# Six constant bf16 products per attention slot, behind the third weighing

## The reference

```
x = x + jnp.tanh(g_xattn[1]) * _L1_xattn_ref(_layernorm(x), ctx_1024, ctx_1024, ...)
x = x + jnp.tanh(g_ffn[1])   * _L1_ffn_ref(_layernorm(x), ...)      # tanh(h W A1 A2 + bias)
x = x + jnp.tanh(g_xattn[2]) * _L2_xattn_ref(_layernorm(x), ctx_1024, ...)
# in both: q, k, v projections, heads of 16, softmax(q k^T / 4) v, output projection
```

## Time and profile before

| what | value |
|---|---|
| median of 3 runs | 1412.94 us |
| lowest and highest run | 1395.23 and 1415.35 us |
| the profiled execution, its own time | 1407.57 us |
| its span in the trace | 1405.8 us |
| PE busy in the span | 1226.4 us, 87% |
| DVE, ACT busy | 716.4 and 450.6 us |
| granted TensorE clock, mean | 0.917 |

### The profile page before, as it was taken

How to read it: one execution, slowest core, us unless ns; L and a number is a source line. 1 busy time by engine, 2 the same in 40 slices (tenths; PEclk the granted TensorE clock), 3 DMA queues, 4 the chain that set the end, 5 groups by cost and what they waited for, 6 DMA issues and landing times.

```text
span 1405.8 us, 19389 instructions
## 1 busy us (share of the span) xinstructions
PE 1226.4 (87%) x6360; PEld 764.1 (54%) x6361; DVE 716.4 (51%) x2061; ACT 450.6 (32%) x842; POOL 293.8 (21%) x347
## 2 busy tenths in 40 slices
PE   6999999999879989998988669999567698999984
PEld 4534434434434443543443649999556446877862
DVE  7263473468966545644752531111376742545557
ACT  3322223123544354444434113333242211333320
POOL 2111111130030011001000041111113662355560
PEclk9999999999987998999998579999876799999997
DMA  9999999100000000000100845555229223455538
GB/s 304 337 337 327 332 335 315 46 1 1 1 0 1 1 1 1 1 1 1 33 1 1 262 145 201 178 175 180 103 77 329 90 91 116 118 152 158 149 108 306
DMA packets 140424, 186.75 MB, mean 133 GB/s; under 512 B 8672, under 2 KB 124896, under 8 KB 140224
## 3 DMA queue, kind: packets, MB, share of 16 engines
q1 hardware_dynamic: 130800, 159.28, 36.8%
q0 software_dynamic: 9552, 26.52, 5.1%
HBM read 83.71 MB, written 102.06 MB: 132 GB/s over the span
## 4 chain that ended last, share of the span: by engine, by line
PE 66%; DVE 15%; issue 7%; ACT 4%; DMA 3%; SPq 2%; POOL 2%; another core or an unknown queue 0%; DVEq 0%; POOLq 0%; ACTq 0%
PE psum L1979 13%; PE psum L1258 6%; PE psum L1269 6%; PE psum L2191 5%; PE psum L2248 3%; PE psum L930 2%; PE psum L2225 2%; PE psum L2272 2%; DVE arena L2810 2%; PE psum L2169 2%; PE psum L1972 2%; PE psum L2007 2%; PE psum L941 2%; ACT xn L1735 2%; PE psum L1933 1%
## 5 line engine op out<-in xcount | busy, mean ns | idle before, releaser
L1979 PE MATMUL psum<-arena 128*128 128x512 f32 x432 | 198.6, 609 | 0.0
L2810 DVE TENSOR_REDUCE arena<-psum 128x4 f32<-128x616 f32 x128 | 101.6, 797 | 100.8 <-PE psum L2191 99.4
L1979 PEld LDWEIGHTS psum<-arena 128*128 128x128 f32 x432 | 80.3, 192 | 113.9 <-issue 113.1
L2191 PE MATMUL psum<-arena 32*128 32x308 f32 x512 | 104.2, 502 | 19.2 <-DVE arena L2810 17.8
L1176 POOL DMA_INDIRECT ys<-xnT,arena x96 | 92.4, 962 | 104.7 <-DVE xnT L1153 82.1
L2392 ACT ACTIVATE arena<-psum,arena 128x512 f32<-128x512 f32 x72 | 49.1, 686 | 166.2 <-PE psum L1979 156.5
L1870 POOL TENSOR_TENSOR x_tok<-x_tok,add_row 128x1024 f32<-128x1024 f32 x16 | 38.3, 2400 | 289.6 <-ACT xn L1735 289.5
L2483 ACT ACTIVATE arena<-psum 128x2048 f32<-128x2048 f32 x40 | 74.9, 1874 | 63.3 <-PE psum L2229 46.6
L1049 PE MATMUL psum<-arena,xn 128*128 x384 | 87.1, 380 | 2.3 <-ACT xn L1099 1.9
L1258 PEld LDWEIGHTS psum<-side,arena 128*128 128x128 f32 x736 | 87.1, 195 | 2.7 <-ACT side L1303 1.6
L1258 PE MATMUL psum<-side,arena 128*128 128x128 f32 x736 | 87.5, 278 | 1.0 <-ACT side L1303 1.0
(11 more groups left out here) (408 smaller groups left out, 2092.6 us busy)
## 6 DMA issues: line engine op xcount, KB each, us to landing
xs<-zeros SPq DMA_DIRECT2D x8, 8576.0 KB, 59.7
arena<-in_W SPq DMA_DIRECT2D x31, 1024.0 KB, 12.0
xn<-xs SPq DMA_DIRECT2D x64, 134.0 KB
arena<-in_gate_up SPq DMA_DIRECT2D x4, 2048.0 KB
arena<-ys SPq DMA_DIRECT2D x4, 2048.0 KB, 14.7
arena<-xs SPq DMA_DIRECT2D x32, 134.0 KB
arena<-in_down SPq DMA_DIRECT2D x4, 1024.0 KB, 5.4
xs<-zeros SPq DMA_DIRECT2D x1, 2990.0 KB, 17.8
```

The costliest lines, as they stand in the source:

```text
L1979: ins = pe.matmul(bank[dict(hn=4, r=5, z=6, xn=7)[k]][:], lhs[:, cols], r, start=(start and n == 0), stop=(stop and n == len(w) - 1))
L2191: ins = pe.matmul(bank[most_bank(n, k) + i][:, 0:2 * M].rearrange("p (h m) -> p h m", h=2), qhT[rows, n % 3, c, t * P:(t + 1) * P], keys[r ...
L2810: dve.tensor_reduce(neg[:, n % 2, t, 2 * pair:2 * pair + 2, 2 * c:2 * c + 2], psum[:, most_bank(n, k):most_bank(n, k) + 2, 0:2 * M].rearra ...
```

## The change

A new operation `fill_wait` stands three times in each slot, between the third weighing and the last one, each time ahead of a maximum step (slot 7 has none of those, but still the operation). PE first waits until ACT has taken the exponential of the third weighing, so that bank 0 is free; then it does two products of the identity with the ternary weights, 128x128 by 128x512 in bf16, into bank 0. Nobody reads them; the last weighing overwrites the bank. That makes six products per slot and 48 in all. DVE and ACT do nothing for the new operation. The core of the diff:

```
             yield ("weigh", n, 2)
             yield from most()
             yield ("untangle", n, 0)
+            yield ("fill_wait", n)
             yield from most()
             yield from ahead("turn", n + 2, 0)
+            yield ("fill_wait", n)
             yield from most()
             yield ("untangle", n, 1)
             yield from ahead("turn", n + 2, 1)
+            yield ("fill_wait", n)
             yield from most()
             yield from token("normalise", 3, tri)
             yield from itertools.islice(second, 1)
...
+            def fill_wait(n):
+                pe.wait_ge(weighed, weighed_at[n, 2] + 1)
+                for _ in range(2):
+                    pe.matmul(bank[0], ident_bf[:], tern.rearrange("p c n -> p (c n)"), start=True, stop=True)
```

More of the change, by code:

```diff
@@ L2319, in mha_tensor @@
                 elif op[0] not in ("tanh", "settle", "normalise", "norm1", "norm2"):
-                    dict(late_turn=late_turn, late_product=late_product, first=first, second=second, turn=turn, query=query, most=most, shift=shift, weigh=weigh, rests=rests, values=values,
+                    dict(fill_wait=fill_wait, late_turn=late_turn, late_product=late_product, first=first, second=second, turn=turn, query=query, most=most, shift=shift, weigh=weigh, rests=rests, values=values,
                          untangle=untangle, back=back, project=project, tri_turn=tri_turn, tri=tri)[op[0]](*op[1:])
@@ L2515, in mha_scalar @@
                     normalise_scalar(act, int(op[0][4]), op[1])
-                elif op[0] not in ("most", "untangle", "project", "tri", "settle", "rests", "finish", "product", "late_product"):
+                elif op[0] not in ("most", "untangle", "project", "tri", "settle", "rests", "finish", "product", "late_product",
+                                   "fill_wait"):
                     dict(late_turn=late_turn, first=first, second=second, turn=turn, query=query, shift=shift, weigh=weigh, values=values, back=back, tri_turn=tri_turn,
```

## The result

The changed kernel took 1453.04 us in the median of four runs (1450.24 to 1456.53), against 1404.53 us (1395.23 to 1415.35) for the kernel before in the same comparison: a ratio of 1.0355, interval 1.0299 to 1.0411, 3.0 to 4.1% slower. The forecast of 1434 us had the sign, but the time is just above the range, which ended at 1452; the second comparison's is inside it.

What follows compares the result with a forecast made beforehand. PE was taken to bound the kernel, with 66% of the chain. The profiled 1407.57 us + 18.9 us for waits and pairs + 6 us for the clock gave 1432.5 us, stated as 1434, range 1414 to 1452.

Steps and rivals of the forecast that it cites:

- The direct price of the waits: Between third and last weighing, PE held until ACT's exponential ends, delaying slots 0 to 7 by 18.9 us at full clock.
- I count nothing as given back: No later wait of the three engines makes up for the delay, so all 18.9 us stay.
- The price of a pair: Two new products hold PE for 0.48 us at full clock (0.43 to 0.54), 0.9 us at the lower clock.
- DVE covers the later pairs: In slots 2 to 5 DVE's 2.22 us between maxima hides pairs two and three, 0.4 us each otherwise.
- The clock term: Extra time at 1.2 GHz behind the new waits: +6 us, bounds a gain of 10 to a loss of 24 us.
- may be part of the same one: In slots 2 to 4, the slow stretch after `tri_turn` merges with one begun before the last weighing, at no added cost.
- one new stretch: Slot 5's clock falls for the first time, for 6.8 us at 1.2 GHz, costing 3.4 us.
- Rival 2: Clock falls in each of slots 0 to 5 through the last weighing: 43 us, 1445 to 1451 us; chance 0.25.
- Rival 3: The pairs hold the clock up among the transposes: 9 us slower, about 1416 us; chance 0.13.
- Rivals 4 and 5: 4: pairs also spare later slow stretches, about 1400 us, chance 0.05. 5: later waits swallow PE's lateness, 1408 us, 0.02.

Runs made afterwards that it cites:

- the second comparison: The unchanged pair, changed kernel against the kernel before, measured again: 1444.34 against 1405.54 us, ratio 1.0287.
- wait_filled: The change plus ten more products into bank 4 ahead of the first wait in slots 0 to 5; ratio 1.0046, seven slots 343.9 us.
- wait_only: The change without its products, keeping the three waits per slot; ratio 1.0105 to the kernel before, seven slots 346.3 us.
- hold_tri: The kernel before plus five products between the two `tri_turn` of slots 2 to 4; ratio 0.9965, seven slots 317.5 us.
- change_hold: The change plus five products between the two `tri_turn` of slots 2 to 4; ratio 1.0288, seven slots 357.2 us.
- exp_first: The kernel before with ACT's exponential ahead of its `normalise`, no products added; ratio 1.0088, seven slots 344.6 us.
- exp_first_pairs: The change with ACT's exponential ahead of its `normalise`; ratio 1.0118, seven slots 338.4 us.
- third_only: The change with only the third `fill_wait` of each slot; ratio 0.994, seven slots 330.8 us.
- pairs_bank4: The change with its products in bank 4 and no wait for the exponential, slots 0 to 6 only; ratio 0.9992, seven slots 338.4 us.
- hold_all: The kernel before plus products between the `tri_turn` and in other existing waits of slots 0, 1 and 6; ratio 0.9891, median 1412.92 us.

## Why the prediction was right and where it was wrong

**The direct price of the waits: right.** Forecast for slots 0 to 6 were 17.0 us at full clock; wait_filled, which has this delay without the change's added time at the lower clock, shows 14.9. It has 5.4 us less at 1.2 GHz in the seven slots than the kernel before; with half of that put back, an estimate, it is 17.6, and the clock's part of the change is 20.8 instead of 23.5. In slot 2 the wait was forecast at 2.6 us and measured at 2.64, and the delay at 2.3 us against 2.4. Slots 3 to 5 came to 3.8, 3.8 and 5.6 us there, but with 3.4, 3.4 and 6.8 us more at 1.2 GHz; less half of that, an estimate, they are 2.1, 2.1 and 2.2 us. Slot 7 was forecast at 1.9 us and took 2.7 and 2.0. "I count nothing as given back" doesn't hold everywhere: slot 2 of wait_only gave all of it back.

**The price of a pair: right.** 0.48 us was taken; five products take 1.14 us in hold_tri (562.02 to 563.16), 0.46 a pair, and in wait_filled a pair takes 0.54 (553.95 to 554.49). At the lower clock 0.9 was taken and 0.96 measured. That DVE covers the later pairs in slots 2 to 5 holds at full clock only.

**The clock term: mis-sized, and the step that failed.** I took +6 us of a range from -10 to +24. Measured is 38.4 - 14.9 = 23.5 us, the upper end. The wrong step is the sentence that the stretch behind `tri_turn` "may be part of the same one; then it has moved and costs nothing more". That merging exists: wait_only shows it in slot 2, where the clock stays down until `query`. In slot 2 of the change the stretch behind the wait has the 10.2 us of wait_only, but the pairs stand in it and push the rest back: the clock is back within the last weighing (573.88, where L2232 takes 0.38 us), `tri_turn` waits its full 1.46 us, and the clock falls again. change_hold shows that the second stretch is a separate one by taking it away. The same happened in slots 3 and 4, where it did not take the products: wait_only falls twice there too, for 6.8 + 6.8 us against 6.8 + 10.2 in the change. So that the pairs split what was one stretch is shown for slot 2 alone.

The rest of the term was missed elsewhere. Over the kernel before, the change has 10.3 us more at 1.2 GHz in each of slots 1 to 4, 13.7 more in slot 5 and 5.7 less in slot 6; at half price, an estimate, that is 15.4 us for slots 2 to 4, 5.1 for slot 1, 6.8 for slot 5 and -2.9 for slot 6. For slot 5 I had one new stretch, 3.4 us. There were two, and the second has nothing to do with `tri_turn`, which slot 5 lacks; it follows a wait for a maximum that the kernel before has too, 0.90 us long, with no fall behind it:

```profile
743.06 0.79 PE L2194 MATMUL psum<-arena 32*128 32x308 f32 x4 [0.90 <-DVE arena L2819]
```

```profile
744.50:751.10 6.60, 6.60 (x29) 1.41 (x22) 1.00 (x2) 1.19 (x2) 1.34 (x5) 0.50 0.00 0
```

Why the clock fell behind it in the change and not before stays open. So the products meant for the clock didn't lower its bill, and of the 11.7 us by which both parts together cost more than the sum of each alone, only the 6.9 us of slot 2 have a cause that the rows show.

**The rivals.** Rival 2 (18.9 + 24 = 43 us, 1445 to 1451) came nearest, in size and in that the clock fell behind the wait in each of slots 0 to 5; the slots took 40 to 41 us more. It didn't have the second fall in slots 2 to 5. It had a chance of 0.25, and the rows spoke for more, though not quite as it says: of the two waits of the earlier trace rows, the one of 1.46 us is shorter than all of the new ones, but that of 3.30 us is longer than the 2.6 us of slots 2 to 5. Rival 3 named something real, as exp_first against exp_first_pairs shows in the seven slots, but the wait of 2.6 to 4 us came before the first product could do anything. Rivals 4 and 5 are out. Of what the prediction weighed from the Trainium skill, page "TensorE: Matmul & The Clock Gate", both sides bear on it. Its part "PE-mode transpose" says that a transpose doesn't count as busy for the clock gate the way a product does, and its section "HAM oscillation" that waits of PE throttle it again. The runs fit the first (products among the transposes, 61 us at 1.2 GHz in exp_first_pairs beside 102 in exp_first) and show the second (wait_only, 96 us beside 65 before), and in this change the second weighed more.

**Left open.** Why the stretches behind `tri_turn` have 6.8 us in slots 3 and 4 of the kernel before and 10.2 in slot 2 and in the same slots of wait_filled wasn't settled; it moves single slots by some 1.7 us. Nor was why whole runs put change_hold no lower than the change, and third_only below the kernel before. That the ratio of the first comparison, 50 us over before, is above the 41 us found in the slots is put down to the differences ahead of slot 0 and behind slot 7 that runs show without any change; it wasn't taken apart further.

## What to carry to other kernels

Work that is meant to keep TensorE's clock up belongs into waits that are already there, into a bank that is free without any further wait: the semaphore that a filler waits on is part of its price, and here it was the larger part (17.3 us for the waits alone, 9.4 for the products alone). Before adding a wait, look up when its releaser ends on its own engine and what stands ahead of it there; PE ran straight into a `normalise` on ACT that had nothing to do with the products. And where a stage repeats, measure it by a landmark in the trace that comes once in each repetition: it agreed within 0.5 us in two profiles of the same kernel where whole runs differed by 20.

## What the runs showed of the hardware

A wait of 1.46 us of PE between transposes was followed by 6.8 to 10.2 us at 1.2 GHz in every slot that had it, of before, the change, pairs_bank4, wait_filled and exp_first alike, and five bf16 products of 0.23 us each within it prevented that in all three slots, in hold_tri, hold_all and change_hold. A wait of 0.90 us for a maximum had 6.8 us behind it in slot 5 of the change and of wait_filled, and none in slot 5 of the kernel before. The stage ahead of the slots runs in more than one way from run to run with the same instructions: between 80 and 200 us of the span the clock was 0.99 in one profile and 0.94 in another, and slot 0 began at 416.3 us with 30.7 us at 1.2 GHz ahead of it, or as late as 430.7 with 60.1. The windows of the kernel before (its second profile) and of the changed one in its first:

```profile
80.00:200.00 120.00, 115.94 (x355) 49.03 (x351) 65.39 (x112) 30.68 (x47) 11.63 (x8) 0.99 1.10 331
```

```profile
80.00:200.00 120.00, 115.94 (x338) 48.97 (x337) 61.79 (x108) 28.73 (x44) 11.63 (x8) 0.94 1.11 333
```

The changed kernel did the one as well as the other (416.3 and 425.9 us), so it is no effect of the change. It is one reason why whole runs couldn't tell a gain of 11.5 us in the slots from none.
